# A chain of four layers on one core: layers 1 to 3 without a setup block of their own

## What is computed

```python
x = x + L0(_gn(x), ...)     # retention-like attention with a decay mask
x = x + L1(_gn(x), ...)     # mLSTM block
x = x + L2(_gn(x), ...)     # 7x7 neighbourhood attention
x = x + L3(_gn(x), ...)     # 7x7 soft-window attention

def _gn(v, G=32, eps=1e-5):
    g = v.reshape(B_, H_, W_, G, C_ // G)
    m = jnp.mean(g, axis=(1, 2, 4), keepdims=True)
    s = jnp.var(g, axis=(1, 2, 4), keepdims=True)
    return ((g - m) / jnp.sqrt(s + eps)).reshape(v.shape)
```

## Time and profile before

| what | us |
|---|---|
| median of 3 runs (lowest, highest) | 3530.23 (3528.97, 3533.43) |
| the profiled execution | 3529.67 |
| its span, first to last instruction | 3527.9 |
| PE busy (share of the span) | 3119.4 (88%) |
| DVE, ACT, POOL busy | 2209.6, 2055.6, 1143.4 |
| layer 1: first weight load issued, first w_up matmul | 1024.66, 1063.14 |
| layer 2: first weight load issued, first value matmul | 2059.44, 2088.07 |
| layer 3: first weight load issued, first gate matmul | 2641.97, 2681.59 |

### The profile page before, as it was taken

One profiled execution on the slowest core, in us unless ns is written; L12 is line 12 of the kernel. 1 busy time (PEld: TensorE's weight loads), 2 busy tenths in 40 slices (PEclk: granted clock), 3 DMA queues, 4 the chain that ended last, 5 costly groups with the idle time before them and its releaser, 6 DMA issues. The chain is left out here.

```text
span 3527.9 us, 94027 instructions
## 1 busy us (share of the span) xinstructions
PE 3119.4 (88%) x38656; PEld 1772.7 (50%) x38656; DVE 2209.6 (63%) x5202; ACT 2055.6 (58%) x4412; POOL 1143.4 (32%) x1446
## 2 busy tenths in 40 slices
PE   6999999999947999999999849999974888888886
PEld 2333333333313565656565527777752666565664
DVE  5877877887724666766676534554444566666665
ACT  3666766766624555555556316665643666676764
POOL 3433443343202222222221112222212455544443
PEclk9999999999967999999999979999997999999998
DMA  6777787778741323332322224544433232333332
GB/s 201 156 172 170 148 184 172 167 151 174 162 132 50 86 65 91 83 82 66 89 70 70 64 97 130 163 149 144 147 109 111 74 101 84 98 102 102 102 95 79
DMA packets 286233, 413.94 MB, mean 117 GB/s; under 512 B 25952, under 2 KB 242800, under 8 KB 264816
## 3 DMA queue, kind: packets, MB, share of 16 engines
q1 hardware_dynamic: 263248, 270.32, 25.7%
q0 software_dynamic: 18432, 134.23, 19.1%
q10 hardware_dynamic: 4128, 3.39, 0.3%
HBM read 219.30 MB, written 53.81 MB: 77 GB/s over the span
## 5 line engine op out<-in xcount | busy, mean ns | idle before, releaser
L732 DVE TENSOR_TENSOR l_probs<-l_psum,l_decay 128x1024 f32<-128x1024 f32 x512 | 598.6, 1219 | 163.3 <-PE l_psum L628 152.6
L780 ACT ACTIVATE l_sizes<-l_probs 128x2048 f32<-128x2048 f32 x256 | 487.0, 1908 | 299.1 <-DVE l_probs L732 291.5
L1793 ACT ACTIVATE l_logits<-l_logits,l_low 128x100 f32<-128x100 f32 x1024 | 373.0, 366 | 272.7 <-DVE l_low L1773 271.6
L1800 POOL TENSOR_TENSOR l_logits<-l_logits,l_inv 128x400 f32<-128x400 f32 x256 | 218.6, 854 | 806.7 <-DVE l_inv L1779 806.2
L628 PE MATMUL l_psum<-l_qk 32*128 32x512 f32 x2048 | 339.5, 645 | 7.5 <-POOL l_qk L866 4.2
L881 POOL DMA_DIRECT2D l_sizes<-l_sizes x128 | 111.2, 869 | 549.3 <-ACT l_sizes L780 537.3
L1632 POOL TENSOR_TENSOR l_E<-l_E,l_causal 128x1024 f32<-128x1024 f32 x64 | 153.3, 2395 | 376.5 <-DVE l_x_act L1365 225.1
L643 PE MATMUL l_psum<-l_probs,l_V 128*32 128x512 f32 x2048 | 269.8, 599 | 1.8 <-DVE l_probs L732 1.6
L1785 DVE COPY l_PT<-l_psum 100x512 f32<-100x512 f32 x256 | 174.9, 683 | 113.4 <-PE l_psum L1746 112.6
L299 PE MATMUL l_psum<-l_xT,l_w_up 128*128 128x512 f32 x512 | 232.0, 607 | 11.9 <-DVE l_row_var L1423 7.8
L1735 PE MATMUL l_psum<-l_keys,l_q_blocks 128*64 128x100 f32 x4096 | 235.2, 257 | 3.7 <-issue 2.3
(11 more groups left out here) (246 smaller groups left out, 6125.2 us busy)
## 6 DMA issues: line engine op xcount, KB each, us to landing
l_sizes<-l_sizes POOLq DMA_DIRECT2D x128, 1024.0 KB, 7.5
l_V_windows<-v_image SPq DMA_DIRECT2D x512, 100.0 KB
l_V_windows<-v_padded SPq DMA_DIRECT2D x512, 100.0 KB
l_E<-rows_c SPq DMA_DIRECT2D x64, 512.0 KB, 5.7
l_xT<-y SPq DMA_DIRECT2D x24, 1024.0 KB, 5.2
y<-l_res SPq DMA_DIRECT2D x32, 512.0 KB, 3.7
l_e_everywhere<-rows_e SPq DMA_DIRECT2D x112, 128.0 KB, 5.5
l_xT<-x SPq DMA_DIRECT2D x8, 1024.0 KB, 11.1
```

What stands on the lines that cost most here:

```text
L732: nc.vector.tensor_tensor(probs[:, N % 2, 2 * p:2 * p + 2, :], ring.region(name).rearrange("p (a n) -> p a n", a=2), decay[:, h:h + 2, s0: ...
L780: nc.scalar.activation(sizes[:, slot(N), :, :], probs[:, N % 2, :, :], ACT.Abs).then_inc(sized, 1)
L1793: nc.scalar.activation(e, e, ACT.Exp, scale=-1.0, bias=self.low[:, N % 4, i:i + 1], accum_out=self.total[:, N % 4, i:i + 1]).then_inc(self ...
L1800: nc.gpsimd.tensor_tensor(p, p, self.inv[:, N % 4, :].unsqueeze(2).to_broadcast([P, STEP, NKEY]), ALU.mult).then_inc(self.p_ready, 1)
```

## The change

`load_all`, the constants' block and the barrier behind it go, in layers 1, 2 and 3; layer 0 keeps its own. What they did is put into the main block:

- SP issues x(0) first, then the large weights, then x(1) and x(2). In layer 1 these two wait until the fold is done (`folded`), since its inputs lie in their tiles. In layer 3 the zeros go out between the weights and x(1), from a cleared key image.
- ACT issues the group mean and the small constants ahead of its table load: 13 loads in layer 1, 4 in layer 2, 10 in layer 3.
- Two semaphores replace the one wait: `first_loaded` (what the norm's average and the first projections need) and `rest_loaded`.
- Layer 1: PE folds behind the norm's first average and ahead of the first w_up, in PSUM banks 6 and 7; DVE makes the constants behind its part of the norm of image 0; ACT copies wq behind the root.
- Layer 2: DVE's two constants come behind its part of the norm, POOL's memset before the variance.
- Layer 3: DVE's memsets come before the statistics, the second key tile first (`keys_cleared`), POOL's memset behind that; the casts and the product come behind DVE's part of the norm, and DVE then waits for `q_cleared` and `cleared`.

```diff
 # layer 1, SP
-                for b in range(3):
+                load(0)
+                sp.dma_start(wup[:, :, :], ktiles(A["L1_WupT"], HALVES)).then_inc(first_loaded, 16)
+                sp.dma_start(back[:, :, :, :].rearrange("p s i n -> p (s i n)"), A["L1_qkvT"]).then_inc(rest_loaded, 16)
...
+                sp.dma_start(wdn[:, :, :], ktiles(A["L1_WdownT"], IT)).then_inc(rest_loaded, 16)
+                sp.dma_start(ident[:, :], A["ident"]).then_inc(rest_loaded, 16)
+                sp.wait_ge(folded, 1)
+                for b in (1, 2):
                     load(b)
 # layer 1, PE
+                def fold():
+
+                    G = 2 * NH
+                    pe.wait_ge(rest_loaded, 272)
+                    for i in range(IT):
+                        c0 = 6 * BANK + i * G
+                        nc.tensor.matmul(PS[:, c0:c0 + G], back[:, 0, i, :], gw[:, 0, i, :], start=True, stop=False)
+                        nc.tensor.matmul(PS[:, c0:c0 + G], back[:, 1, i, :], gw[:, 1, i, :], start=False, stop=True)
...
+                    m.then_inc(folded, 1)
+
+                pe.wait_ge(first_loaded, 32)
                 for u, t in layer1_steps():
                     N = u * CHUNKS + t
+                    if u == -2 and t == 1:
+                        fold()
+                    if u == -1 and t == 0:
+                        pe.wait_ge(wq_ready, 1)
+                        pe.wait_ge(consts_ready, 1)
 # layer 1, DVE
+                def constants():
+                    G = 2 * NH
+                    nc.vector.memset(eps[:, :], ROOT_EPS * 1e-6)
...
+                    dve.wait_ge(rest_loaded, 272)
+                    heads = wv[:, :, :].rearrange("p i (r d) -> p i r d", r=2)
+                    vstep(dve, nc.vector.tensor_reduce(wmean[:, :, :], heads, axis=AX.X, op=ALU.add))
...
+                    dve.wait_ge(folded, 1)
+                    nc.vector.tensor_copy(wg[:, :, 0:G], PS[:, 6 * BANK:6 * BANK + 2 * IT * G].rearrange(
+                        "p (i n) -> p i n", n=G)).then_inc(consts_ready, 1)
+                    dve.wait_ge(consts_ready, 1)
                         norm.moments(nc, dve, vstep, b)
                         norm.collect(nc, dve, ring, b)
+                        if u == -2:
+                            constants()
 # layer 1, ACT
+                act.dma_start(norm.group_mean[:, :], A["group_mean"]).then_inc(first_loaded, 16)
...
+                    act.dma_start(dst, src).then_inc(rest_loaded, 16)
                         norm.root(nc, act, u // 2 + 1)
+                        if u == -2:
+                            act.wait_ge(folded, 1)
+                            nc.scalar.activation(wq[:, :, :].rearrange("p i n -> p (i n)"), PS[:, 7 * BANK:8 * BANK], ACT.Copy,
+                                                 scale=DH ** -0.5).then_inc(wq_ready, 1)
+                            act.wait_ge(consts_ready, 1)
 # layer 1, POOL
                             apply(b)
+                            if u == -2:
+                                pool.wait_ge(consts_ready, 1)
 # layer 2, SP
+                load(0)
+                sp.dma_start(wqkv[:, :, :], A["L2_WqkvT"].rearrange("(k p) n -> p k n", k=HALVES)).then_inc(first_loaded, 16)
+                sp.dma_start(wo[:, :, :], A["L2_WprojT"].rearrange("(k p) n -> p k n", k=HALVES)).then_inc(rest_loaded, 16)
...
+                for b in (1, 2):
                     load(b)
 # layer 2, PE, DVE, ACT, POOL
+                pe.wait_ge(first_loaded, 32)
                 norm.average(nc, pe, ring, 0)
...
+                pe.wait_ge(rest_loaded, 96)
...
+                dve.wait_ge(rest_loaded, 96)
+                nc.vector.tensor_scalar(qkv_b[:, 0:HALVES], qkv_b[:, 0:HALVES], HD ** -0.5, None, ALU.mult).then_inc(bias_ready, 1)
+                vstep(dve, nc.vector.tensor_tensor(bias[:, :, :], bias[:, :, :], window[:, :, :], ALU.add))
...
+                act.wait_ge(bias_ready, 1)
+                act.wait_ge(q_cleared, 1)
...
+                nc.gpsimd.memset(w.q[:, :, :, :], 0.0).then_inc(q_cleared, 1)
+                pool.wait_ge(q_cleared, 1)
                 norm.variance(nc, pool, pstep, ring, 0)
 # layer 3, SP
+                load(0)
+                sp.dma_start(wqkv[:, :, :], in_halves(A["L3_WqkvT"])).then_inc(first_loaded, 16)
+                sp.dma_start(wo[:, :, :], in_halves(A["L3_WoutT"])).then_inc(rest_loaded, 16)
+                sp.wait_ge(keys_cleared, 1)
+                for s in range(2):
+                    zeros = keys[1][:, :, :].rearrange("p g n -> p (g n)")
+                    sp.dma_start(vimg[s].rearrange("n c -> (n c)").rearrange("(p n) -> p n", p=P), zeros).then_inc(cleared, 16)
+                for b in (1, 2):
                     load(b)
                 for half in range(2):
                     spread_args(0, half)
+                sp.wait_ge(cleared, 32)
 # layer 3, DVE
+                nc.vector.memset(keys[1][:, :, :], 0.0).then_inc(keys_cleared, 1)
+                nc.vector.memset(eps4[:, :], 4e-6)
+                nc.vector.memset(all_mean[:, :], 1.0 / C)
+                nc.vector.memset(keys[0][:, :, :], 0.0)
+                vstep(dve, nc.vector.memset(outside[:, :], 0.0))
                 norm.moments(nc, dve, vstep, 0)
                 norm.collect(nc, dve, ring, 0)
+                dve.wait_ge(rest_loaded, 144)
+                nc.vector.tensor_copy(outside[0:16, :], soft[0:16, 0, :])
+                nc.vector.tensor_copy(pick[:, :], osq[:, 0, 0:64])
+                nc.vector.scalar_tensor_tensor(w_qk[:, 0:1], w_qk[:, 0:1], HD ** -0.5 / GAIN, w_qk[:, 1:2], ALU.mult,
+                                               ALU.mult).then_inc(consts_ready, 1)
+                dve.wait_ge(consts_ready, 1)
+                dve.wait_ge(q_cleared, 1)
+                dve.wait_ge(cleared, 32)
 # layer 3, POOL
+                pool.wait_ge(keys_cleared, 1)
+                nc.gpsimd.memset(w.q[:, :, :, :], 0.0).then_inc(q_cleared, 1)
+                pool.wait_ge(q_cleared, 1)
                 norm.variance(nc, pool, pstep, ring, 0)
```

More of the change, by code:

```diff
@@ L1460, in residual @@
                                             ring.region(name).rearrange("p (m n) -> p m n", m=HALVES), ALU.add).then_inc(ring.took(name), 1)
+                def constants():
+                    G = 2 * NH
+                    nc.vector.memset(eps[:, :], ROOT_EPS * 1e-6)
+                    nc.vector.memset(ones[:, :], 1.0)
+                    nc.vector.memset(ends[:, :, :], 0.0)
+                    nc.vector.memset(xm[0][:, :, 0:TAPS - 1], 0.0)
+                    nc.vector.memset(wg[:, :, :], 0.0)
+                    vstep(dve, nc.vector.memset(v1[:, :, :, :], 0.0))
+                    for r in range(2):
+                        nc.vector.memset(v1[:, :, :, :].rearrange("p s (i r) d -> p s i r d", r=2)[:, :, :, r, DH + r], 1.0)
+                    dve.wait_ge(rest_loaded, 272)
+                    heads = wv[:, :, :].rearrange("p i (r d) -> p i r d", r=2)
+                    vstep(dve, nc.vector.tensor_reduce(wmean[:, :, :], heads, axis=AX.X, op=ALU.add))
+                    vstep(dve, nc.vector.tensor_scalar(wmean[:, :, :], wmean[:, :, :], 1.0 / DH, 0.0, ALU.mult, ALU.add))
+                    nc.vector.tensor_tensor(heads, heads, wmean[:, :, :].unsqueeze(3).to_broadcast([P, IT, 2, DH]), ALU.subtract)
+                    dve.wait_ge(folded, 1)
+                    nc.vector.tensor_copy(wg[:, :, 0:G], PS[:, 6 * BANK:6 * BANK + 2 * IT * G].rearrange(
+                        "p (i n) -> p i n", n=G)).then_inc(consts_ready, 1)
+                    dve.wait_ge(consts_ready, 1)
                 conv_steps = 0
@@ L1900, in store @@
                     sp.dma_start(y[b, :, :, s], norm.x(b)[:, :, s]).then_inc(stored, 16)
-                for b in range(3):
+                load(0)
+                sp.dma_start(wqkv[:, :, :], A["L2_WqkvT"].rearrange("(k p) n -> p k n", k=HALVES)).then_inc(first_loaded, 16)
+                sp.dma_start(wo[:, :, :], A["L2_WprojT"].rearrange("(k p) n -> p k n", k=HALVES)).then_inc(rest_loaded, 16)
+                sp.dma_start(bias[:, :, :].rearrange("p k n -> p (k n)"), A["L2_bias"]).then_inc(rest_loaded, 16)
+                sp.dma_start(window[:, :, :].rearrange("p k n -> p (k n)"), A["window"]).then_inc(rest_loaded, 16)
+                for b in (1, 2):
                     load(b)
@@ L2389, in _ @@
                             unit(unit_name(u, -1))
+                pe.wait_ge(rest_loaded, 144)
+                pe.wait_ge(consts_ready, 1)
+                pe.wait_ge(q_cleared, 1)
                 for j in range(8):
```

141 lines of the change are left out of this document (37 added, 104 removed).

## The result

| kernel | median (lowest, highest), runs | ratio to the kernel before, 95% interval |
|---|---|---|
| before | 3531.83 (3528.97, 3543.88), 4 | |
| changed | 3481.93 (3477.25, 3500.06), 4 | 0.9862 [0.9820, 0.9904] |

What follows compares the result with a forecast made beforehand. Layer heads, closed off by all-engine barriers, were taken as the local bound: 16.6 + 16.5 + 24.6 = 57.7 us saved in layers 1 to 3, giving 3472.5 us, range 3466 to 3483.

Steps and rivals of the forecast that it cites:

- The lengths of the layers behind these points should be those of now within a microsecond: Sign in the changed profile: behind each layer's first matmuls after the head, layer lengths stay unchanged within a microsecond.
- the lower bound: Layer 1, loading before the fold: 12.7 us, supposing the tail of tiny loads goes under the bulk.
- the upper side: Layer 1, loading before the fold: upper bound 15.8 us, extra bytes on top of 13.24; 14.7 was taken.
- signs of being wrong: A DVE memset much over 2.5 us, averaging matmul waiting on a load, DVE waiting for zeros, or changed body length.
- The first two steps: Layer 3's head: statistics at 6.5 us after the first issue, bound by DVE's memsets; first matmul at 15.0 us.
- The wait on cleared is the new one to look at: Layer 3: DVE's wait for the zeros before its first gate read, held covered by 1.9 us.
- the 24.6 us of the sum: Layer 3's head: first matmul at 2657.0 instead of 2681.59, 24.6 us saved.
- Late head: Rival: weights delay x(0), or DVE's keys memset waits for POOL's; 9.0 of 57.7 us go, 3481.5; chance 0.20.
- It doesn't do what it says: Rival: SP's queue alone has half the rate, so loads come back as waits; 18.2 us go, 3490.7; chance 0.06.
- Warmer and smoother: Rival, layer 1: w_up runs at full clock straight after the fold, and loads take 13.6; 3469.5; chance 0.12.
- Slower than before: Rival: shorter pauses between layers move 65 us of loop work to TensorE's low clock, using up the gain; chance 0.03.
- The weighed rule on DVE beside a POOL memset: Heads: memsets and statistics on DVE don't lock the port shared with GpSimd, so DVE's work beside POOL's memset costs nothing.

Runs made afterwards that it cites:

- fold_waits: Changed kernel, layer 1: fold operands loaded right behind x(0), TensorE waiting before the fold for these two alone; ratio to before 0.9837, median 3473.60.
- before_again: The kernel before, unaltered, measured once more against itself; ratio 1.0001, median 3535.00 beside 3533.17.
- best: Changed kernel with the edits of own_waits and fold_waits, and layer 3's second keys memset behind the norm's collection; ratio to before 0.9826, median 3473.49.
- own_waits: Changed kernel, layer 3: VectorE waits only for the small loads it reads, and for the cleared images later; ratio to before 0.9841, median 3475.52.
- cleared_moved: Changed kernel, only layer 3's VectorE wait for the cleared images moved behind the gate units, ahead of the key scaling; one run of 3476.93.
- x_after_zeros: Changed kernel, layer 3: SP waits until both images are cleared before loading x(1) and x(2); one run of 3474.91.
- best_pool: As best, but GpSimd no longer waits for VectorE's first keys memset before its own memset in layer 3; ratio to before 0.9815, median 3470.20.

## Why the prediction was right, and where it was wrong

**Where the time is.** Right: what the diff touches is the heads, and nothing reached beyond them that would show against the bodies' own spread. "The lengths of the layers behind these points should be those of now within a microsecond" was wrong as a test, since they differ by up to 22 us between two executions of the same kernel; no single profile could have passed it.

**Layer 1.** Right in every number: the fold's first matmul at 14.9 us (14.7), the fold of 7.0 (7.16), w_up straight behind it, 16.6 saved (16.6). That the wait for all 17 loads sets it is shown by fold_waits. But that 14.7 came so close is in part luck. SP's loads were in at 12.8 us, where the lower bound has 12.7, and the 2.1 us behind them were seven small loads on ACT's queue, 1036.8 to 1038.6: the tail that the lower bound supposed to go under the bulk. The prediction went to the upper side for another reason, the 323 GB/s of the first nine microseconds (339 in the changed kernel). The same tail is what it missed in layer 3. One of its signs of being wrong did show in layer 1, for nothing: the averaging matmul waited some 0.3 us for w_up (it came 3.66 us behind the start of the statistics, 3.33 in fold_waits).

**Layer 2.** The first value matmul came at 13.0, not 12.1. x(0) landed as taken (5.06 for 5.0); the chain from the statistics to the first matmul took 7.94 us for 7.09. Of that 0.7 is in POOL's four applies, 3.73 us beside DVE's bias sum (2058.88) where the same form took 3.02 in layer 3. The bias sum overlaps these applies by 0.8 us; that it is the cause is argued, not isolated. The prediction let POOL's applies meet only the two casts of layer 3. To the first score matmul 16.3 us are saved of 16.5, and that is luck: the value matmuls took 9.26 instead of the 9.98 of the earlier trace rows. The rows of the granted clock say why: it went from 0.50 to 1.00 4.3 us into the 32 matmuls, and 5.7 us into them in the kernel before. In before_again it did so after 3.0 us, they took 8.61, and against that profile the head is only 14.7 us shorter.

**Layer 3.** The first two steps held: statistics at 6.56 (6.5), bound by DVE's memsets, with PE at 15.3 (15.0); best shows that the memsets were the bound. The step that failed is "The wait on cleared is the new one to look at". In front of DVE's first gate read stand two waits for DMAs, and only one was priced. The other, for rest_loaded, was treated nowhere as a term: for layer 3's ten small loads on ACT's queue the prediction has no landing time at all. In the profile of before w_on landed 4.4 us after its issue, but there the two large weights had been in for 1.8 us by then and no bulk came behind them; here 5.82 MB went by. Its price, worked out from the changed kernel and own_waits: the read at 24.0 instead of 20.1 or less, PE 3.6 us late, then 24 matmuls in 8.01 instead of 5.46, and less by 0.2 later: 5.9 us (own_waits). The wait for the cleared images, which was priced, was too optimistic as well (landed 17.9 us after the first issue, at 2626.9; 14.8 to 16.4 forecast), and cost nothing (cleared_moved), for the read had more cover than the prediction gave it: 20.1 at least and not 18.3. So the 24.6 us of the sum came out as 16.7 (15.9 on before_again): 5.9 of the missing 7.9 are this wait and what followed from it.

**The other 2 us of the 8.** own_waits is still 22.6 us shorter than before and not 24.6. The first gate matmul is 0.3 to 0.5 us later than forecast; the gate matmuls take 5.85 us where they took 4.97 in the earlier trace rows; the rest is in the first key means. In the nine profiles of kernels without the setup block, these 32 gate matmuls took between 5.0 and 6.4 us: the granted clock went from 0.50 to 1.00 2.8 us into them where they took 5.00 (cleared_moved), 4.6 where 5.89 (changed), 5.7 where 6.42 (x_after_zeros), and 2.7 in the kernel before. So this term is the clock's. Why the rise comes where it does is left open.

**The clock.** The prediction let the clock in as a rival for the loops and not as a follow-up cost of a wait in a head. Its effect is seen in layer 3 in nine profiles: PE stood for 3.15, 3.22, 3.69 and 4.30 us between gate and value matmuls in four of them, and the 24 value matmuls took 6.85, 8.44, 8.01 and 7.11 us; in the five in which it didn't stand they took 5.46 each time. The row of 2630 to 2632 above shows a granted clock of 1.00 when the pause began, that of 2634 to 2640 0.57 behind it: it was at the 1.2 GHz level from 2632.3, while PE stood, to 2639.1. In the four profiles with a pause the value matmuls ran for 2.9 to 6.1 us at that level, and about half of this is what they took longer, 1.4 to 3.0 us; the length of the pause doesn't order them (after 4.30 us of pause they took 1.65 longer, after 3.22 they took 2.98 longer). A wait that held PE 3.6 us cost 5.9 in all in this pair of profiles.

**The rivals.** "Late head" gave 3481.5, within a microsecond of the first comparison, and for none of its reasons: DVE's memsets waited for no memset of POOL's, x(0) landed at 5.1 in layer 2, the fold began within its bounds. Its price was right by accident. "It doesn't do what it says" fell: the fold began at 14.9 and the images were cleared 17.9 us after the first issue, where half the rate of one queue wanted 20.8 and 26.7. (Its term for layer 2, 11.8 us, counts ACT's bytes as well, which the other two don't; by their rule it is 11.2. Nothing hangs on it.) "Warmer and smoother" fell too: w_up's first sixteen matmuls took 8.48 us (8.72 before). "Slower than before" found nothing: the bodies of both kernels lie in one band. The weighed rule on DVE beside a POOL memset held, with 2.46 us beside one of 6.92 in best_pool.

## What to carry to other kernels

Where several loads count on one semaphore, price the wait by the last of them as it will land beside its new neighbours, not by what the waiting engine reads; give early readers a semaphore of their own, and put small loads ahead of bulk in time, not only on another queue. List every wait in front of an instruction, not only the new one that looks dangerous. And when a kernel's time jitters by more than the effect, measure between two fixed instructions in the trace: here the ratio's interval was 30 us wide, and the heads repeated within 0.7 us in the changed kernel and 1.6 in the kernel before. Of two terms that came out right, one (layer 1) hid the tail of small loads that made the third wrong, and the other (layer 2) was helped by the clock: check what a wait ended on, and not only when.

## What the runs showed that was not expected

- Small loads beside bulk on the other queue: w_on (1 KB) landed 18.5 us after its issue, 13.3 with x(1) and x(2) held back, 4.7 with the zeros held back too. Microsecond by microsecond the two queues moved the same number of packets, 36 and 38 where one side's were of 11.5 KB.
- A pause of PE of 3 to 4 us in front of 24 matmuls made them 1.4 to 3.0 us longer, on top of the pause: the granted clock had gone from 1.00 to 0.50.
- Two executions of the same kernel differ by 22 us in the bodies of three layers. TensorE's granted clock over layer 1's body, the same code in all profiles, was between 0.94 and 0.96, while the busy time of ACT and POOL in it stayed within 2 us and DVE's within 13.
